# Causal attention: the weighted sums of two neighbouring key steps issued together, at the second of the two

## The reference

```
logits = q @ k.T / sqrt(8)
logits = where(k_pos > q_pos, -inf, logits)
attn = softmax(logits)
out = (attn @ v) @ W_out + b_out
x = x + out;  x = x + ffn(layernorm(x))
```

## Time and profile before

| | |
|---|---|
| median of 3 runs | 1576.52 us (1567.07 to 1581.94) |
| the profiled execution | 1573.21 us, its span 1571.4 us, mean granted clock 0.965 |
| PE busy | 1438.6 us (92%) |
| DVE busy | 1235.9 us (79%) |
| ACT busy | 980.0 us (62%) |
| causal layer's attention with what leads up to it, 880 to 1475 us of the span | PE 549.54, DVE 445.55, ACT 354.78 us busy |

### The profile page before, as it was taken

The page is one execution under the profiler, slowest core; times in us unless marked ns, Lnnn a source line. Parts: engine busy times, 40 slices in busy tenths (PEclk is TensorE's granted clock), DMA queues, the critical chain, the costliest instruction groups (busy, mean ns, idle before and its releaser), DMA issues.

```text
span 1571.4 us, 26128 instructions
## 1 busy us (share of the span) xinstructions
PE 1438.6 (92%) x9625; PEld 701.7 (45%) x9625; DVE 1235.9 (79%) x3106; ACT 980.0 (62%) x1259; POOL 108.9 (7%) x210
## 2 busy tenths in 40 slices
PE   3699999999999999999988988999999999999888
PEld 2444344434444443444436654444444444444455
DVE  7589999999999998999937757787787877777254
ACT  4427777777777777777774432666666666666622
POOL 6020000000000000000001112000000000000010
PEclk9859999999999999999999985999999999999999
DMA  3720111111101111110001323111121112210000
GB/s 95 221 57 7 27 28 29 29 29 28 28 6 25 28 28 29 28 28 2 2 1 54 83 79 76 35 29 29 29 53 32 29 29 47 38 29 2 8 21 27
DMA packets 40055, 58.39 MB, mean 37 GB/s; under 512 B 7796, under 2 KB 19448, under 8 KB 39928
## 3 DMA queue, kind: packets, MB, share of 16 engines
q1 hardware_dynamic: 39928, 56.72, 15.2%
HBM read 36.77 MB, written 18.87 MB: 35 GB/s over the span
## 4 chain that ended last, share of the span: by engine, by line
PE 70%; DVE 18%; ACT 5%; issue 4%; DMA 2%; SPq 1%; POOL 0%; DVEq 0%; ACTq 0%; POOLq 0%
PE psum L995 25%; PE psum L1045 23%; DVE maxima L785 11%; PE psum L1009 6%; PE psum L1142 5%; PE psum L938 4%; ACT probs L559 3%; DVE junk L782 3%; PE psum L1147 2%; PE psum L1017 1%; PE psum L948 1%; DVE xn L706 1%; PE psum L1062 1%; DMA k_parts<-parts 1%; DMA qop<-shift_rows 1%
## 5 line engine op out<-in xcount | busy, mean ns | idle before, releaser
L559 ACT ACTIVATE probs<-psum 128x1024 f32<-128x1024 f32 (+3 forms) x896 | 794.2, 932 | 300.4 <-PE psum L1009 192.7
L785 DVE TENSOR_REDUCE maxima<-psum 128x1 f32<-128x512 f32 x1280 | 815.2, 684 | 72.8 <-PE psum L995 67.8
L995 PE MATMUL psum<-kop,qop 62*128 62x512 f32 (+3 forms) x1792 | 657.0, 465 | 56.5 <-DVE maxima L782 20.0
L1009 PE MATMUL psum<-qop,kop 64*128 64x512 f32 (+3 forms) x1792 | 498.2, 411 | 10.4 <-ACT probs L559 7.8
L995 PEld LDWEIGHTS psum<-kop,qop 62*128 62x128 f32 x1792 | 289.6, 191 | 487.6 <-DVE maxima L785 325.4
L1045 PE MATMUL psum<-probs,vwin 128*32 128x512 f32 (+3 forms) x3584 | 441.6, 565 | 3.9 <-ACT probs L559 2.0
L782 DVE CUSTOM_DVE_ANT_0 junk<-psum,mask 128x384 bf16<-128x384 f32 (+3 forms) x512 | 237.4, 487 | 75.3 <-PE psum L995 69.8
L1009 PEld LDWEIGHTS psum<-qop,kop 64*128 64x128 f32 x1792 | 242.0, 189 | 55.7 <-ACT probs L559 44.7
L1045 PEld LDWEIGHTS psum<-probs,vwin 128*32 128x32 f32 x3584 | 71.8, 109 | 105.5 <-issue 84.6
L1017 PE MATMUL psum<-half_ident,key_mask 64*128 64x64 bf16 x1024 | 92.7, 198 | 0.0
L1142 PE MATMUL psum<-ffn_xt,wffn 128*128 128x512 f32 x192 | 87.6, 594 | 0.0
(11 more groups left out here) (88 smaller groups left out, 709.9 us busy)
## 6 DMA issues: line engine op xcount, KB each, us to landing
qop<-q_parts SPq DMA_DIRECT2D x256, 64.0 KB
q_parts<-parts SPq DMA_DIRECT2D x32, 256.0 KB, 3.0
k_parts<-parts SPq DMA_DIRECT2D x32, 256.0 KB, 3.4
kop<-k_parts SPq DMA_DIRECT2D x64, 128.0 KB
kop<-k_parts SPq DMA_DIRECT2D x128, 64.0 KB
x<-in_L_attn_a_x SPq DMA_DIRECT2D x8, 256.0 KB, 4.4
qop<-shift_rows SPq DMA_DIRECT2D x128, 8.0 KB
out_x<-x SPq DMA_DIRECT2D x8, 256.0 KB, 2.3
```

Source lines behind the costliest of these rows:

```text
L559: nc.scalar.activation(probs[:, slot, :, c0:], psum[:, bank:bank + 2, c0:], ACT.Exp, scale=SCORE_SCALE).then_inc(probs_ready, 1)
L785: nc.vector.tensor_reduce(dst, src, AX_X, ALU.max).then_inc(ring_free, 1)
L995: mm(psum[:, slot, 0:width], qop[rows, buf, f, r, qb * P:(qb + 1) * P].bitcast(F32R), kop[rows, buf, r, kh * CHUNK:kh * CHUNK + width].bit ...
L1009: ins = mm(psum[:, bank + h, c0:], kop[rows, buf, pair, j * P:(j + 1) * P].bitcast(F32R), qop[rows, buf, f, pair, c0:].bitcast(F32R), star ...
```

## The change

In the causal layer, a call for the weighted sums of a step is put on a list. When two are on the list, or when the step is the last of a half, all that are listed are issued one behind the other. The non-causal layer keeps one at a time. Since a half has an even number of steps, the pairs are (0,1), (2,3), ... (10,11), and the first of each pair is issued one position later than before: position 0 issues the sums of steps 0 and 1, position 2 of 2 and 3, and so on to position 10; the odd positions issue none.

```
+        self.sums_together = 2 if causal else 1
...
+                due_sums = []
+
+                def queue_sums(w, buf, s, unit):
+
+                    due_sums.append((w, buf, s, unit))
+                    if len(due_sums) == plan.sums_together or s in plan.half_end:
+                        for step in due_sums:
+                            weighted_sums(*step)
+                        due_sums.clear()
...
                             elif part == 2:
-                                weighted_sums(w + prev[0], (buf + prev[0]) % BUFS, prev[1], prev[2])
+                                queue_sums(w + prev[0], (buf + prev[0]) % BUFS, prev[1], prev[2])
...
                         if s and pair:
-                            weighted_sums(0, 0, s - 1, unit - 3)
+                            queue_sums(0, 0, s - 1, unit - 3)
...
-                weighted_sums(last, last_buf, plan.n - 1, prev[2])
+                queue_sums(last, last_buf, plan.n - 1, prev[2])
```

## The result

The changed kernel took 1599.87 us (median of 4 runs, 1599.57 to 1603.76) against 1575.61 before: ratio 1.017, 95% interval 1.0138 to 1.0203. It is slower. Its profiled span is 1598.3 us against 1571.4, 26.9 us more.

A forecast was written before the change was run, and what follows sets the result against it. PE, DVE and ACT passing a short queue to and fro were taken as the bound. A turn gets 1.0 us longer, 15 x 1.0 = +15 us, so 1573.2 + 15 = 1588.2, forecast 1588; range 1562 to 1608.

The forecast's parts named there:

- no change: Whole kernel: a time within about 1% (15.8 us) of the one before; chance 0.57.
- rival 2: Position 11 loses its long work, PE idles, clock halves: four to eight turns of 2.5 us, 1598 to 1608; chance 0.14.
- Position 11 and 0: Removing step 0's sums at 11 gains nothing; at position 0 they delay position 1's first job by 0.88 us, starving DVE.
- Positions 1 to 3: Delay +0.69 after DVE's 0.19 gap, +1.13 with step 2's sums, +0.13 once position 3 has no sums.
- Position 5: Without step 6's sums, DVE stays full and only its 0.57 gap is won: delay +1.01 falls to +0.44.
- the walk: Position-by-position count of PE's or DVE's delay through a causal turn: each turn 1.0 us longer, +15 us in all.
- The boundary of two sums: On PE, between two steps' joined sums: cost from 0 to 0.33 us, taken as 0.
- rival 3: A pair's second weight loads wait for the first's matmuls: +15 us on the walk, 1603; chance 0.09.
- The entry from row tiles to the full transpose: PE's tiling change into the norm transpose at position 3: cost 0 to 0.21 us, taken as 0.21.
- Rival 1: PE is the bound and each pair gains up to 0.33 us: 1551 or 1564, at its fullest 1543; chance 0.22.
- falling waits of job loads for DVE: Sign against the forecast, which expected PE's job loads to wait for DVE above 6.2 us a turn.
- DVE's total idle time: Sign over a turn: the forecast is wrong if this shrinks; no size given.

The follow-up runs named there:

- first_pair_only: Kernel before the change with only the sums of steps 0 and 1 joined: 1601.04 us, ratio 1.0184.
- its twin with the unread sums: Kernel before with only steps 0 and 1 joined, plus 8 matmuls at position 11 like the removed sums, result unread: 1578.66 us, one run.
- pair_8_only: Kernel before the change with only the sums of steps 8 and 9 joined: 1575.99 us, one run.
- pair_10_only: Kernel before the change with only the sums of steps 10 and 11 joined: 1573.53 us, ratio 0.9987.
- pairs_4_and_10: Kernel before the change with only the sums of steps 4 and 5 and of steps 10 and 11 joined: 1568.56 us, ratio 0.9968.
- unread_sums_at_11: The whole change plus, at position 11, the same 8 matmuls as the removed sums of step 0, result unread: 1595.02 us, ratio 1.0123.

## Why the prediction was wrong

**The direction of the mechanism was right, the sum was not.** I forecast 1588 us, less than 1% over the time before, and gave 0.57 to "no change". It is 1.7% slower.

**The step that failed** is the one that left the clock out of the sum: "A turn thus gets 1.0 us longer: 15 x 1.0 = +15 us". The mechanism stood among the rivals, as rival 2, with a chance of 0.14 and four to eight turns of 2.5 us. Measured are 13 turns of 14, each with 1.55 us. It is the larger part of the loss: 20.2 us less the 2.5 of before, against 9.8 for the turns' own length. first_pair_only and its twin with the unread sums show it alone: 14 turns disturbed against none, 1601.04 against 1578.66 us. I had seen the cover go, and gave it little weight. What I did not consider is that the turn repeats: what lets the clock fall in one turn stands in each.

The row that I leaned on for rival 2 does not bear it. The one stretch of before begins 5.1 us into its turn, at position 1, with the sums of positions 11 and 0 in place, and lasts 6.8 us; the stretches of position 0 begin at 2.9 to 4.1 us and last 3.4, hence 1.55 us a turn and not 2.5. And that turn was not like the others: DVE stands in it for 0.27 us, 3.4 us in, where the profile shows nothing that it waits for.

```profile
1105.84 0.29 DVE L782 CUSTOM_DVE_ANT_0 junk<-psum,mask 128x128 bf16<-128x128 f32 x1 [0.27 <-issue]
```

The same 0.27 stands at that place in the fourth of the 14 turns in every one of the 14 traces, and makes the turn longer at full clock too: 32.23 us in pair_8_only against 31.95 for the next. Whether it brought the stretch on is not shown. That rival 2 named the right place is in part luck, and so is its 1598 to 1608, which holds the measured time only because more turns lost less each.

**The rival's reason was not exact either.** "PE is idle" was not enough: three job matmuls in the idle time did not keep the clock, eight matmuls of the removed kind did. Which property of theirs decides was not tried: they differ in number, shape, tiling and operands, and run for 1.07 us against 0.94. And rival 2 named position 11 alone; position 5, left without sums, does the same in 4 turns of the whole change and in 6 of 14 when position 11 is cured.

**Position 11 and 0** were right: nothing won at 11 (the shift transpose stayed at POOL's heels), +0.81 instead of +0.88 at the first job of position 1, DVE starved for 1.03 us.

**Positions 1 to 3** came out somewhat too dear: at the norm transpose I had +0.13, measured is -0.04. Of these 0.17, 0.07 were there at position 1 already, and DVE won back 0.28 (0.81 to 0.53) where I had counted only the written idle time of its gap (0.19). **Position 5** adds less than 0.1: at the start of position 6 the walk had +0.44, measured is +0.16, but +1.01 against +0.81 had come in from position 4, and DVE won back 0.65 in a gap written as 0.57. The rest is carried along: the second scores of position 8 were then +0.66 forecast, +0.34 measured, and the end +1.0 forecast, +0.70 measured. The form of the walk, up by a step at each even position and back at each odd one until DVE or ACT holds PE, is what the trace shows.

**The unknown costs.** The boundary of two sums at 0 was right (1.74 for two). So rival 3 is out, and with it the rule of the Trainium skill ("TensorE: Matmul & The Clock Gate", Part 3, What overlaps and what doesn't) that loads overlap only in other row groups. The trace disagrees, and the measurement decides: the second step's loads stand at 1291.18 and 1291.61, on all 128 rows, while the matmuls from 1290.72 on still run. The entry from row tiles to the full transpose at 0.21 gave the place of the norm transpose to 0.2 us.

**Rival 1**, PE alone as the bound, is out: 30.2 us a turn were its mark, and three of the four middle pairs lengthen the turn. The rule of the Trainium skill on tiling modes ("TensorEngine Tiling (Array Packing)", Key Properties) is not what failed, since the two joined sums follow without a drain; but what PE saves it spends at the odd positions in waits for DVE or ACT. The 0.33 us of a pair shows in full only in the largest gain, (10,11).

**What I had said would show me wrong**: falling waits of job loads for DVE. The wait for the masked maxima fell, from 6.2 to 4.3 us, and I had expected it above 6.2. By that sign I was wrong, although the unmasked waits made up for it (7.3 to 7.0 together). As evidence it was badly chosen: where DVE is starved, the wait moves from PE's loads to DVE (4.1 to 5.7). The sign beside it, DVE's total idle time, did not shrink: the turn less DVE's busy time is 7.84 us against 6.68.

**What stays open**: which property of the matmuls holds the clock; and why pair_10_only had four turns with a stretch at about 6 us, near where the kernel before had its one and pairs_4_and_10 had none. The four kernels with a stretch that begins 5 to 7 us into a turn all have one in the fourth turn; the seven others that keep the sums at position 11, or have unread ones there, have none.

## What to carry to other kernels

A matmul that stands in a wait is free, and moving it out of the wait makes it cost its full length elsewhere; look for what covers an operation before asking what its new neighbour saves. Between engines that pass a short queue, bunching work on one of them starves the others, so join only where the followers have slack: here two of six pairs, 0.3% faster, where all six were 1.7% slower. A loop repeats whatever lets the clock fall: if a change takes PE's long matmuls away from a place in a loop, put the price of a disturbed turn (1.55 us here) times the number of turns into the sum. And before a single disturbed turn of the trace of before is taken as a sign, look at where in the turn its stretch begins.

## What the runs showed of the hardware that was not expected

Eight matmuls whose result nobody reads made a kernel 22 us faster (1601.04 to 1578.66 us, the second a single run), because the granted clock stayed at 2.4 GHz in all 14 turns. That is still slower than the kernel before, 1574.33 us on that chip.

A disturbed turn tends to be followed by one disturbed at the same place: in first_pair_only all 14, starting 3.3 to 3.8 us into the turn in 13 of them, and turns of 33.75 to 34.2 us. The undisturbed turns of unread_sums_at_11 likewise come in a row, the last seven, 32.43 us each. The number of disturbed turns may therefore be a property of a run as much as of a kernel: pairs_4_and_10 ran from 1564.31 us, at a mean granted clock of 0.966, to 1575.37, at 0.957.
